# Storing and multiplying the second layer's graph messages as high and low f16 halves

## The reference, cut to what matters

```python
def gcn_conv(x, row, col, ew, W, b):            # row = source, col = destination, with self loops of weight 1
    deg = segment_sum(ew, col, num_segments=n)
    dis = where(deg > 0, rsqrt(deg), 0)
    h = x @ W.T
    return segment_sum(h[row] * (dis[row] * ew * dis[col])[:, None], col, num_segments=n) + b

def block(x, g, bln, W, b):
    return x + relu(gcn_conv(layer_norm(x, g, bln), row, col, ew, W, b))

xn = layernorm(x)
gnn = block(block(xn, layer 1), layer 2) @ Wp.T + bp
x = x + gnn + mix(xn)                           # mix: linear attention over all nodes, 8 heads, and an MLP
x = x + ffn(layernorm(x))                       # 8 experts 256 -> 512 -> 256, gelu, the 2 best by gate are summed
```

## Time and profile before

| | |
|---|---|
| median of 3 runs | 5193.85 us (5193.22 to 5195.35) |
| the profiled execution | 5195.25 us, span 5193.5 us, mean granted PE clock 0.901 |
| busy share of the span | PE 75%, PE weight loads 63%, POOL 59%, DVE 49%, ACT 23% |
| gathers, L571 | 3126, 2996.8 us busy, 959 ns each |
| message matmuls, f32 | 7028 records, 1857.2 us, 414 ns each |
| scatter operations, L1098 | 3514, 988.8 us, 357 ns each |
| chain that ended last, by engine | PE 31%, another core or an unknown queue 28%, issue 22%, ACT 10%, DVE 7% |
| DVE idle before its first operation of layer 1's first window (300.96 us) | 20.55 us |
| DMA | 525.71 MB, 101 GB/s over the span |

### The profile page before, as it was taken

How to read it: one execution, slowest core, us unless ns; L and a number is a source line. 1 busy time by engine, 2 the same in 40 slices (tenths; PEclk the granted TensorE clock), 3 DMA queues, 4 the chain that set the end, 5 groups by cost and what they waited for, 6 DMA issues and landing times.

```text
span 5193.5 us, 89964 instructions
## 1 busy us (share of the span) xinstructions
PE 3896.0 (75%) x27204; PEld 3252.7 (63%) x27205; DVE 2524.4 (49%) x8946; ACT 1187.1 (23%) x3161; POOL 3080.2 (59%) x3315
## 2 busy tenths in 40 slices
PE   6847666766766766676658888888888888888888
PEld 4735555555555555555547777776777777777777
DVE  8734444444444444444434554454554554454554
ACT  3500000000000000000013333333333333333334
POOL 3266666666666666666645666666665666566662
PEclk9968877788888888888879999999999999999999
DMA  3333333333333333333323333333333333333331
GB/s 135 129 108 110 108 110 114 108 108 112 109 107 113 111 109 109 113 110 108 113 74 94 94 94 92 95 95 91 97 93 93 93 95 96 92 94 93 93 94 42
DMA packets 269256, 525.71 MB, mean 101 GB/s; under 512 B 62088, under 2 KB 168080, under 8 KB 269200
## 3 DMA queue, kind: packets, MB, share of 16 engines
q0 software_dynamic: 150144, 410.19, 27.0%
q1 hardware_dynamic: 119056, 114.93, 6.7%
HBM read 471.66 MB, written 53.22 MB: 101 GB/s over the span
## 4 chain that ended last, share of the span: by engine, by line
PE 31%; another core or an unknown queue 28%; issue 22%; ACT 10%; DVE 7%; SPq 1%; DVEq 1%; DMA 0%; ACTq 0%; POOL 0%; POOLq 0%
PE bank L1320 30%; ACT bank L732 5%; DVE ss L1098 2%; PE bank L1342 2%; ACT L732 1%; ACT L715 1%; ACT w L735 1%; DVE w L1222 1%; DVE rstd L752 1%; DVE rstd L751 0%; ACT hT L700 0%; DVE rstd L753 0%; DVE u L769 0%; DVEq L1098 0%
## 5 line engine op out<-in xcount | busy, mean ns | idle before, releaser
L571 POOL DMA_INDIRECT gs<-h_d,src_row x3126 | 2996.8, 959 | 1866.1 <-PE bank L1320 881.6
L1320 PE MATMUL bank<-gs,ss 128*128 128x256 f32 x7028 | 1857.2, 414 | 31.2 <-issue 15.2
L1320 PEld LDWEIGHTS bank<-gs,ss 128*128 128x128 f32 x7028 | 1431.2, 211 | 264.0 <-issue 55.3
L1098 DVE TENSOR_SCALAR ss<-iw,dst_all,ew_all 128x128 f32<-128x128 f32 x3514 | 988.8, 357 | 760.6 <-PE bank L1320 549.2
L1320 PE MATMUL bank<-experts,w 128*128 128x256 f16 x4848 | 605.8, 277 | 289.7 <-DVE w L1222 286.3
L1222 DVE SCALAR_TENSOR_TENSOR w<-bank,w 128x512 f16<-128x512 f32 x404 | 278.9, 690 | 1000.1 <-ACT w L735 923.8
L1320 PE MATMUL bank<-w,experts 128*128 128x128 f16 x9696 | 641.0, 220 | 126.1 <-issue 115.4
L732 ACT ACTIVATE bank<-bank,eb1c 128x128 f32<-128x128 f32 x1616 | 450.2, 341 | 1184.6 <-remote 1100.2
L1320 PEld LDWEIGHTS bank<-experts,w 128*128 128x128 f16 x4848 | 458.5, 99 | 391.3 <-issue 320.4
L1320 PEld LDWEIGHTS bank<-w,experts 128*128 128x128 f16 x9696 | 575.1, 98 | 185.5 <-issue 158.9
L1342 PE MATMUL bank<-ident,u 128*128 128x128 f32 x596 | 147.5, 336 | 497.6 <-DVE u L769 370.9
(11 more groups left out here) (272 smaller groups left out, 3085.0 us busy)
## 6 DMA issues: line engine op xcount, KB each, us to landing
gs<-h_d,src_row POOLq DMA_INDIRECT x3126
hself<-self_d SPq DMA_DIRECT2D x100, 128.0 KB
ew_in<-in_eW SPq DMA_DIRECT2D x49, 168.0 KB
out<-u SPq DMA_DIRECT2D x51, 128.0 KB
u<-xn_d SPq DMA_DIRECT2D x50, 128.0 KB
h_d<-u SPq DMA_DIRECT2D x50, 128.0 KB
self_d<-u SPq DMA_DIRECT2D x50, 128.0 KB
u<-x_d SPq DMA_DIRECT2D x50, 128.0 KB
```

What stands on the lines that cost most here:

```text
L571: pool.indirect_dma_start(gs[:, n, :], None, table[:, :], bass.IndirectOffsetOnAxis(ap=src_row[:, c:c + 1], axis=0), element_offset=P * D) ...
L1098: m = dve.tensor_scalar(ss[:, u % S_SLOTS, :], iw[:, :], dst_all[:, c], ew_all[:, c], ALU.is_equal, ALU.mult)
L1320: return pe.matmul(out_ap, lhsT, rhs, start=first, stop=last, **kw)
```

## The change

The weights and the second table are held as f16 halves, and each use of layer 2 becomes three f16 matmuls:

- The table `h2_d` has rows of 512 f16 (256 high, 256 low), still 1 KB. ACT writes the high half of the row tile behind `u4`, DVE the low half in piece 6 of `window1`; both into `row_halves`, which SP writes out once DVE is done. `self2_d` stays f32 and is written first.
- The edge weights are multiplied by 1024 at the start, in place, on DVE. Behind the first five scatter groups of layer 1 DVE splits them: the high part by an f16 copy, the low part by a subtraction into `ew_low_all`, in two pieces of 1024 and 552 columns, four operations in a chain.
- Layer 2's scatter group writes two f16 matrices for each use, with the weight and with its low part, into the same slot of `ss`. It compares an f16 row of 0 to 127 with `near`, the window's 36 columns of destination minus first node, which `set_window` makes for layer 2 instead of `iw`.
- The scales come out in `dis1` = dis / 1024 for layer 1 and `dis2` = dis / (1024 x 256) for layer 2; the self term of layer 1 goes through an identity times 1024.
- `over` for layer 2 does the same with halves; its sum is scaled as it is added. `gs`'s last two slots are set to zero between the layers, so that f32 leftovers are not read as f16, and PE waits for it.
- Three more constants on POOL; the columns of the edge arrays go from 1568 to 1576; the memory of three weight matrices is shared with `ew_low_all`.

The diff, cut to its core:

```diff
-        h2_d = nc.dram_tensor("h2_d", [(W + 2) * P, D], F32).ap()
+        h2_d = nc.dram_tensor("h2_d", [(W + 2) * P, 2 * D], F16).ap()
...
 SP, window1
                 sp.wait_ge(s["h2_done"], w + 1)
-                sp.dma_start(h2_d[bass.ds(here, P), :], u4[:, :]).then_inc(s["h2_out"], 16)
                 sp.dma_start(self2_d[bass.ds(here, P), :], u4[:, :]).then_inc(s["h2_out"], 16)
+                sp.wait_ge(s["h2_low"], w + 1)
+                sp.dma_start(h2_d[bass.ds(here, P), :], row_halves[:, :, :].rearrange("p a d -> p (a d)")
+                             ).then_inc(s["h2_out"], 16)
                 sp.wait_ge(s["x1_done"], w + 1)
...
 ACT, next_h_scaled
                 act.activation(u4[:, :], wide(7), ACT.Copy, scale=dis[:, bass.ds(w, 1)]).then_inc(s["h2_done"], 1)
+                act.wait_ge(s["h2_done"], w + 1)
+                act.activation(row_halves[:, 0, :], u4[:, :], ACT.Copy, scale=ROW_UP).then_inc(s["h2_high"], 1)
...
 DVE, phase 0
             dve.wait_ge(s["pool_links"], EDGE_LINKS)
+            dve.tensor_scalar(ew_all[:, :], ew_all[:, :], EW_UP, None, ALU.mult)
             dve.memset(k_sum[:, :], 0.0).then_inc(s["k_summed"], 1)
...
             dve.wait_ge(s["dis_set"], len(CUTS) - 1)
+            dve.tensor_scalar(dis1[:, :], dis[:, :], 1.0 / EW_UP, None, ALU.mult)
+            dve.tensor_scalar(dis2[:, :], dis[:, :], 1.0 / (EW_UP * ROW_UP), None, ALU.mult)
...
 DVE, scatter_group
-                    m = dve.tensor_scalar(ss[:, u % S_SLOTS, :], iw[:, :], dst_all[:, c], ew_all[:, c], ALU.is_equal, ALU.mult)
+                    if layer == 0:
+                        m = dve.tensor_scalar(ss[:, u % S_SLOTS, :], iw[:, :], dst_all[:, c], ew_all[:, c],
+                                              ALU.is_equal, ALU.mult)
+                        continue
+                    for half_of, part in ((0, ew_all), (1, ew_low_all)):
+                        m = dve.tensor_scalar(ss_h[:, u % S_SLOTS, half_of, :], iota_h[:, :], near[:, u:u + 1], part[:, c],
+                                              ALU.is_equal, ALU.mult)
...
 DVE, set_window, layer 2
+                    m = dve.tensor_scalar(near[:, :], dst_all[:, bass.ds(at + (FRONT - SIDE), USES)],
+                                          win_first[:, bass.ds(node_w, 1)], None, ALU.subtract)
...
 DVE, behind the first scatter groups of layer 1
+            for c in range(0, DCOL, piece_of):
+                n = min(piece_of, DCOL - c)
+                ch.link(dve.tensor_copy(high[:, 0:n], ew_all[:, c:c + n]))
+                ch.link(dve.tensor_tensor(ew_low_all[:, c:c + n], ew_all[:, c:c + n], high[:, 0:n], ALU.subtract))
+            def rows_low():
+                return dve.scalar_tensor_tensor(out=row_halves[:, 1, :], in0=u4[:, :], scalar=ROW_UP,
+                                                in1=row_halves[:, 0, :], op0=ALU.mult, op1=ALU.subtract)
...
 DVE, window1
+                    if k == 6:
+                        dve.wait_ge(s["h2_high"], w + 1)
+                        rows_low().then_inc(s["h2_low"], 1)
...
 DVE, between the layers
             window1(W - 1, last=True)
+            dve.wait_ge(s["h2_high"], W + 1)
+            rows_low().then_inc(s["h2_low"], 1)
+            dve.memset(gs[:, SLOTS - SIDE:SLOTS, :], 0.0).then_inc(s["blank_set"], 1)
...
 PE, messages
-                    m = mm(acc, ss[:, u % S_SLOTS, :], gs[:, n, :], layer == 1 and u == 0, True, skip_group_check=True)
+                    if layer == 0:
+                        m = mm(acc, ss[:, u % S_SLOTS, :], gs[:, n, :], False, True, skip_group_check=True)
+                    else:
+                        for a, b in HALVES:
+                            m = mm(acc, ss_h[:, u % S_SLOTS, a, :], gs_h[:, n, b, :], u == 0 and (a, b) == HALVES[0], True,
+                                   skip_group_check=True)
```

More of the change, by code:

```diff
@@ L45 @@
 FRONT = 8
-NCOL = -(-(NCH + 1) // 8) * 8
+NCOL = -(-(CH * W + SIDE) // 8) * 8
 NO_EDGES = NCH
@@ L81 @@
 LATE = NE // 2
-N_CONSTS = 26
+N_CONSTS = 29
 TURN = 6
@@ L146, in gps_kernel @@
         ew = ew_all[:, FRONT:DCOL]
-        w6 = sb("w6", [P, KB, D]); w7 = sb("w7", [P, KB, D]); wp = sb("wp", [P, KB, D])
-        wq = sb("wq", [P, KB, D]); wk = sb("wk", [P, KB, D]); wv = sb("wv", [P, KB, D]); wm = sb("wm", [P, KB, D])
+        ew_low_all = sb("ew_low_all", [P, DCOL])
+        w6, wk, wv = (ew_low_all[:, i * KB * D:(i + 1) * KB * D].rearrange("p (k n) -> p k n", k=KB) for i in range(3))
+        assert 3 * KB * D <= DCOL
+        w7 = sb("w7", [P, KB, D]); wp = sb("wp", [P, KB, D])
+        wq = sb("wq", [P, KB, D]); wm = sb("wm", [P, KB, D])
         w1 = sb("w1", [P, 2 * KB, HID]); w2 = sb("w2", [P, HBLK, D])
@@ L340, in _ @@
             sp.wait_ge(s["consts"], N_CONSTS)
-            for table, b in ((xn_d, W), (h1_d, 0), (h1_d, W + 1), (h2_d, W + 1), (self1_d, W + 1), (self2_d, W + 1), (x1_d, W),
-                             (r_d, 0)):
+            for table, b in ((xn_d, W), (h1_d, 0), (h1_d, W + 1), (self1_d, W + 1), (self2_d, W + 1), (x1_d, W), (r_d, 0)):
                 sp.dma_start(rows(table, b), zero_tile[:, :]).then_inc(s["blank_out"], 16)
+            sp.dma_start(rows(h2_d, W + 1), zero_tile[:, :].bitcast(F16)).then_inc(s["blank_out"], 16)
             def tile(t, b):
@@ L559, in over @@
                     pool.indirect_dma_start(
-                        go[:, :], None, table[:, :],
-                        bass.IndirectOffsetOnAxis(ap=idx_o[:, 0:1], axis=0), element_offset=P * D).then_inc(s["over_in"], 16)
+                        go[:, :] if layer == 0 else go_h.rearrange("p a d -> p (a d)"), None, table[:, :],
+                        bass.IndirectOffsetOnAxis(ap=idx_o[:, 0:1], axis=0),
+                        element_offset=P * D * (layer + 1)).then_inc(s["over_in"], 16)
             def gathers(layer, table):
@@ L1120, in window1 @@
                         dve.wait_ge(s["main_set"], v + USES)
-                        set_window(0, w + 1, w + 1)
-                        scatter_group(v_next, 0, at_next)
+                        set_window(int(last), 0 if last else w + 1, w + 1, at_next)
+                        scatter_group(int(last), v_next, 0, at_next)
                     if k == 6:
-                        scatter_group(v_next, 1, at_next)
+                        scatter_group(int(last), v_next, 1, at_next)
                     if k == 0:
@@ L1158, in window1 @@
                     if k + 5 < GROUPS:
-                        scatter_group(v, k + 5, at, uses)
-                scatter_group(v_next, 2, at_next)
+                        scatter_group(0, v, k + 5, at, uses)
+                scatter_group(int(last), v_next, 2, at_next)
                 dve.wait_ge(s["main_used"], v + USES + S_SLOTS)
-                dve.scalar_tensor_tensor(out=t_b[1][:, :], in0=acc, scalar=dis[:, bass.ds(w + 1, 1)], in1=vec[:, 0, :],
+                dve.scalar_tensor_tensor(out=t_b[1][:, :], in0=acc, scalar=dis1[:, bass.ds(w + 1, 1)], in1=vec[:, 0, :],
                                          op0=ALU.mult, op1=ALU.add).then_inc(s["acc_read"], 1)
-                scatter_group(v_next, 3, at_next)
+                scatter_group(int(last), v_next, 3, at_next)
                 dve.wait_ge(s["acc_read"], w + 1)
@@ L1241, in window2 @@
                     if msgs and k + 4 < GROUPS:
-                        scatter_group(v, k + 4, at, uses)
+                        scatter_group(1, v, k + 4, at, uses)
                     if msgs and k == 3:
@@ L1290, in window2 @@
                     dve.wait_ge(s["self2_done"], w + 1)
-                    dve.scalar_tensor_tensor(out=u7[:, :], in0=acc, scalar=dis[:, bass.ds(w + 1, 1)], in1=hself[:, :],
+                    dve.scalar_tensor_tensor(out=u7[:, :], in0=acc, scalar=dis2[:, bass.ds(w + 1, 1)], in1=hself[:, :],
                                              op0=ALU.mult, op1=ALU.add).then_inc(s["acc2_read"], 1)
                     if not last:
-                        scatter_group(v_next, 3, at_next)
+                        scatter_group(1, v_next, 3, at_next)
                     dve.wait_ge(s["acc2_read"], w + 1)
@@ L1452, in over @@
                     pe.wait_ge(s["over_in"], (base + t) * 16 + 16)
-                    mm(wide(4), so[:, :], go[:, :], True, True).then_inc(s["over_used"], 1)
+                    if layer == 0:
+                        m = mm(wide(4), so[:, :], go[:, :], True, True)
+                    else:
+                        for a, b in HALVES:
+                            m = mm(wide(4), so_h[:, a, :], go_h[:, b, :], (a, b) == HALVES[0], (a, b) == HALVES[-1])
+                    m.then_inc(s["over_used"], 1)
                 pe.wait_ge(s["over_links"], over_step(layer, base, n, 0))
```

73 lines of the change are left out of this document (49 added, 24 removed).

## The result

The changed kernel takes 5282.86 us (median of 4 runs, 5280.43 to 5290.95), the kernel before 5194.6 us in the same comparison: ratio 1.0172, 95% interval 1.0154 to 1.0190. Forecast were 5155 us and a gain. The profiled execution has a span of 5281.4 us, 87.9 more than before. It splits by the starts of two lines that stand once in each window, the reading of the message sum in layer 1 (L1163 before, L1218 after; in the trace of before it runs from 350.7 to 2634.1) and in layer 2 (L1291, now L1349).

The account below looks back on a forecast made before the run. POOL's gathers were taken to pace layer 2, not PE. From 5195.25 us, -40.5 in layer 2 and +2.0 once gave 5156.7, or 5155 against the median; own range 5138 to 5182, whole range 5040 to 5232.

Parts of the forecast that it names:

- The slots keep POOL's pace: Layer 2: in 47 of 49 windows POOL's four gathers plus handing over set the 6.13 us slot, not PE.
- What counts is the stretch 3645.95 to 3652.31 ... up to 1.0 us per window.: PE's message saving counts only between two layer 2 windows: up to 1.0 us per window, 0.8 taken.
- Scatter on DVE: Layer 2: two f16 operations replace each f32 one, 0.20 us each (0.17 to 0.25), hidden in slots, just in time at window's end.
- The last window: Layer 2's last window, where PE does bind: 29 uses at 0.10 us less, 2.9 us gained.
- Layer 1 at 0, once-only costs +1.5 and +0.5: Layer 1's added operations cost nothing; start-up edge-weight and scale work +1.5 us (0.5 to 3); between layers +0.5.
- the cover of the two new operations: Layer 1's added ACT copy and DVE operation stand in idle stretches of 11.71 and 4.83 us; without cover 24 us.
- the prediction's own sign: If layer 1's period grows at all, the idle cover named for its added ACT and DVE operations was wrong.
- the 9.02 us of POOL's wait: Between layers, POOL's wait for the overflow step hides the later table, leaving 2 us or none; +0.5 taken.
- Rival C: Layer 2: doubled scatter operations lengthen POOL's gathers, slower by 44 us, near 5237; chance 0.11.
- Rival D: Layer 2: more PE idle time lowers its clock, costing 1.7 us near each window's end, 5236; chance 0.10.
- Rival A: Layer 2: PE's whole message saving counts, slots follow PE, 172 us gained, 5023; chance 0.12.

Follow-up runs that it names:

- b_split3: Kernel before with each layer 2 f32 message matmul cut into two of 128 columns, on a holding chip: 5245.6 us, ratio 1.0203.
- b_double: Kernel before with a second scatter operation per use in layer 2, into memory nothing reads, holding chip: 5148.5 us, ratio 1.0002, one run.
- a_two: Changed kernel with two of three products in layer 2 (low weights times high rows left out), holding chip: 5204.0 us, ratio 1.011, one run.
- a_four: Changed kernel with a fourth product in layer 2, low weights with low rows, holding chip: 5270.6 us, ratio 1.0252 to the kernel before.
- a_late: Changed kernel with scatter groups 2 and 3 moved behind x2 at layer 2's window end, holding chip: 5230.3 us, ratio 1.0166 to the kernel before.
- a_again2: The changed kernel itself once more, as reference on another holding chip: 5242.7 us, ratio 1.0186 to the kernel before.
- a_half2: Changed kernel writing only the weights' high half in layer 2 (36 scatter operations per window), same PE matmuls, holding chip: 5219.1 us, ratio 1.0148.
- p_before2: Kernel before with plain copies instead of indirect gathers in layer 2, holding chip: 4655.7 us, ratio 0.905, one run.
- a_norows: Changed kernel without layer 1's two new row-half operations, table written as zeros without the wait, chip that does not hold: ratio 1.0053.
- a_half: Changed kernel writing only the weights' high half in layer 2, same PE matmuls, chip that does not hold: 4294.7 us, ratio 0.9996.
- b_first: Kernel before with the message sum read and x2 made ahead of expert 6's addition, chip that does not hold: ratio 1.0013.
- p_before: Kernel before with plain copies instead of layer 2's indirect gathers, chip that does not hold: 4286.7 us, one run.
- p_after: Changed kernel with plain copies instead of layer 2's indirect gathers, chip that does not hold: 4212.7 us, one run.
- a_wide: Changed kernel with one 512-column and one 256-column matmul per use, high-low left out of the sum, chip that does not hold: ratio 1.0071.
- a_first: Changed kernel with scatter groups 2 and 3 and also expert 6's addition moved behind x2, holding chip: 5179.0 us, ratio 1.0064.
- b_split: Kernel before with each layer 2 f32 message matmul cut into two of 128 columns, chip that does not hold: ratio 1.0021.

## Why the prediction was wrong, step by step

*The slots keep POOL's pace.* Right on the chips it was read from: 6.16 us, with 0.4 us less of message work on PE in each. PE's saving of 217 us became idle time. But it is a trait of the holding chips together with indirect gathers, not of the kernel: elsewhere POOL gathers without a break, and with plain copies PE binds on both kinds.

*"What counts is the stretch 3645.95 to 3652.31 ... up to 1.0 us per window."* **This step failed.** I let results of PE at the window's end be acted on at once, though I had just found that in the slots they are not. The stretch of matmuls got shorter by 0.9 us, as counted. But expert 6's addition, between its output and the next messages, starts 2.72 us behind that output in the mean, before 0.72: 2.0 us lost for 0.9 won. With the smaller changes in the slots and in the gathers the period grew by 1.54 us, where I had it shrink by 0.8, and 48 periods took 73.7 us more, where I had 37.6 less. In the kernel before, the result mostly got through before POOL's run was over; in the changed one it does not.

I had also priced the change's matmuls by array time alone, 0.33 against 0.43 us per use, and their number at nothing. b_split3 shows that this was wrong: it changes only how each f32 matmul is cut, and costs 2.0%. Is it their number, then? On holding chips the ratios are: one f32 matmul per use 1.000 (1.0002 with DVE doubled), two in f32 1.0203, two in f16 1.011, three 1.0186, four 1.0252. Array time can't order these (0.43, 0.45, 0.22, 0.33 and 0.44 us, the f16 ones at 0.11 a matmul). But the number of matmuls as written can't either, since two in f32 cost more than three in f16. What orders them is the number of records in the trace, where an f32 matmul has two: per use 2 (period 49.31, b_double), 2 in f16 (50.01), 3 (50.75, or 50.44 with half the scatter work), 4 in f32 (51.16), 4 in f16 (51.43). The two with 2 records differ by 0.7 us (a_two also has the doubled scatter work), so it is not all.

A rival was not tested: *when* within a gather the output ends. In the kernel before and in b_double expert 6's output ends 0.10 us behind the start of the run's last gather in nearly every window. In the 8 late windows of the kernel before it is 0.15 to 0.16 us in five and 0.10 in three; none of the others has it at 0.15 or 0.16. In a_four it ends 0.20 and in b_split3 0.27 us behind that start, and is late in 45 of 46. A delay of 0.1 us could thus be enough, whatever makes it. Against this as the whole cause: in a_late the output ends 0.57 us ahead of that start in both the late windows and the others. (The ends of matmuls are modelled here from their starts, in all kernels alike.)

*Scatter on DVE.* 0.22 us from start to start, where I took 0.20 between 0.17 and 0.25. The group ahead of the low half made the second output later than I had allowed (0.96 us, not 0 to 0.4), but this is the smaller part on holding chips: a_late removes it and keeps most of the loss (1.0166, against 1.0186 in a_again2 and 1.0172), and a_half2 gives back 0.4%.

*The last window.* 5236.0 - 5199.44 = 36.6 us (the last two starts of L1349), 37.1 before: -0.6, not -2.9.

*Layer 1 at 0, once-only costs +1.5 and +0.5.* Measured 5.2 in layer 1, 5.2 ahead of it and 4.2 between the layers. On the two other holding chips layer 1 costs more: six traces of changed kernels have 2283.3 to 2294.0 us for its 48 periods, three with the layer 1 of before (b_double, p_before2, b_split3) 2267.2 to 2275.4, some 16 us less. So the cover of the two new operations was not there, as the prediction's own sign says, though DVE and ACT idle where they stand; which wait they lengthen is open. On chips that do not hold, the same comparison gives 1 us, within the spread, and a_norows, without the two operations, is 4 us below the shortest. The 4.2 between the layers was called hidden behind the 9.02 us of POOL's wait; it is not wholly hidden.

*Rival C,* longer gathers, is false where the forecast was made (946 against 960 ns) and true on the other kind, at 0.51 us per window against a_half. Against b_first, which has the scatter work of before and a period of 40.20, it is 0.33. *Rival D,* the clock, is false: 0.99. The times of C and D, 5237 and 5236, were the nearest to the measured one, by mechanisms that did not act. Rival A is in part what p_before and p_after show, without indirect gathers, at 74 us of its 172.

The Trainium skill ("SBUF — State Buffer", Who interferes with whom) has a DVE operation in a two-port mode and a GpSimd one exclude each other. The traces don't bear a full block out: 36 operations of 0.22 us more per window, 8 us, lengthened the gathers by 0.5 us where they run without a break, and not at all on a holding chip (946 ns in a_again2, 951 in a_half2 with half of the operations). Whether these operations run in such a mode, no run here shows.

**What stays open:** what it is in an indirect gather that holds PE's results on some chips, and why the gap at the window's end closes when there are more PE instructions. It may be their number per microsecond, their sum, or the moment in the gather at which the output ends; no run separates these. a_wide, with two matmuls per use and unchanged array time, would have told something of the number, but ran on no holding chip. No version beats the kernel before: a_first is the best of the changed ones, and b_first wasn't tried on a holding chip.

## What to carry to other kernels

When one matmul is replaced by several, don't price it by array time alone: beside indirect gathers on the holding chips, nearly the same array time in twice the matmuls cost 2.0%. Look at every window and not at one: the kernel before was late in 8 of 46, the changed one in 45. Before an idle engine's saving is booked anywhere, ask of each wait on the chain when its releaser's result was seen, not when its matmuls ended. And time a change on more than one chip: the same pair gave 1.017 and 1.007 here, with different bounds.

## What the runs showed of the hardware

The same kernel takes 5145 to 5195 us on some chips and 4295 to 4301 us on others. On the first, most results of PE are acted on only 1.0 to 1.2 us after a run of indirect gathers is over (hidden group to gelu in the slots shown: 4.2 to 4.4 us). Some get through during the run, as expert 6's in the kernel before. On the second kind this wait is not there: in a_half and b_split the addition starts 0.28 us behind its output, in all but a few of 46 windows, though the gathers run without a break. With plain copies from the same queue both have a period of 39.78 us in layer 2, and in the slot shown the gelu follows its group by 0.04 us.
